# Graph network: the attention's logits with features on the partitions instead of edges

## The reference, cut to what matters

```
x_l = (x @ W_l).reshape(n, H, C)
x_r = (x @ W_r).reshape(n, H, C)
e = (ea @ W_e).reshape(-1, H, C)
m = jax.nn.leaky_relu(x_l[src] + x_r[dst] + e, NEG_SLOPE)
alpha = jnp.einsum('ehc,hc->eh', m, att)
amax = jax.ops.segment_max(alpha, dst, num_segments=n)
expa = jnp.exp(alpha - amax[dst])
denom = jax.ops.segment_sum(expa, dst, num_segments=n)
a = expa / (denom[dst] + 1e-16)
out = jax.ops.segment_sum(x_l[src] * a[:, :, None], dst, num_segments=n)
```

## Time and profile before

| what | us |
|---|---|
| median of the three runs | 2528.77 |
| span of the profiled execution (first to last instruction) | 2249.7 |
| what lies around the span (the median less the span; the profile has no time of its own for the execution) | 279.1 |
| first to last gather of the attention | 984.6 to 2142.2 |
| last logits of the last group done | 2150.4 |

### The profile page before, as it was taken

One profiled execution on the slowest core, in us unless ns is written; L12 is line 12 of the kernel. 1 busy time (PEld: TensorE's weight loads), 2 busy tenths in 40 slices (PEclk: granted clock), 3 DMA queues, 4 the chain that ended last, 5 costly groups with the idle time before them and its releaser, 6 DMA issues. The chain is left out here.

```text
span 2249.7 us, 34161 instructions
## 1 busy us (share of the span) xinstructions
PE 1665.0 (74%) x10041; PEld 1359.7 (60%) x10041; DVE 1504.7 (67%) x3141; ACT 969.8 (43%) x2263; POOL 916.3 (41%) x880
## 2 busy tenths in 40 slices
PE   5566666899799999865667677766777767776756
PEld 2455555655478887634566666666666656666744
DVE  4766666577744342477677777867777867787875
ACT  0355565677455234430234434434434335344535
POOL 1000000000100000037777777777777777777800
PEclk9555555799999999988788988888888898898877
DMA  2100000000034000034333333333343333333211
GB/s 70 60 1 1 1 1 1 8 0 0 29 87 130 27 1 6 14 100 96 92 90 91 97 93 91 92 96 92 87 100 94 86 95 97 91 93 93 60 39 29
DMA packets 134433, 136.86 MB, mean 61 GB/s; under 512 B 28689, under 2 KB 105074, under 8 KB 134258
## 3 DMA queue, kind: packets, MB, share of 16 engines
q0 software_dynamic: 27776, 60.71, 12.2%
q1 hardware_dynamic: 106482, 73.98, 11.5%
HBM read 129.67 MB, written 4.92 MB: 60 GB/s over the span
## 5 line engine op out<-in xcount | busy, mean ns | idle before, releaser
L2112 POOL DMA_INDIRECT rows<-x_l,src x856 | 896.9, 1048 | 292.5 <-issue 260.1
L2180 PE MATMUL psum<-both,node_hot 128*128 128x144 f32 x1712 | 304.1, 332 | 202.0 <-DVE both L2374 175.2
L2180 PEld LDWEIGHTS psum<-both,node_hot 128*128 128x128 f32 x1712 | 264.7, 222 | 229.4 <-issue 197.4
L2127 PE MATMUL psum<-w_e,edges 128*128 128x272 f32 x856 | 323.9, 466 | 56.7 <-DVE z L2287 46.9
L2129 PEld LDWEIGHTS psum<-x_r,hot 128*128 128x128 f32 x1712 | 313.8, 224 | 51.1
L2129 PE MATMUL psum<-x_r,hot 128*128 x1712 | 313.1, 312 | 0.0
L2287 DVE TENSOR_TENSOR z<-psum,rows 128x544 f32<-128x544 f32 x214 | 154.3, 721 | 235.4 <-issue 163.7
L2237 ACT ACTIVATE apart<-iota,minus_rel 128x128 f32<-128x128 f32 x828 | 261.9, 386 | 0.0
L769 ACT ACTIVATE counts<-psum (+1 forms) x181 | 181.5, 1003 | 175.8 <-PE psum L762 112.1
L1145 POOL TENSOR_TENSOR ht<-ht,mix_rows 128x512 f32<-128x512 f32 (+1 forms) x7 | 7.8, 1149 | 587.4 <-ACT mix_rows L1186 587.4
L1260 PE MATMUL psum<-halves,counts 128*128 128x257 f16 (+1 forms) x1725 | 198.1, 277 | 7.4 <-DVE halves L1465 3.9
(11 more groups left out here) (335 smaller groups left out, 2187.3 us busy)
## 6 DMA issues: line engine op xcount, KB each, us to landing
rel_row<-e_rel_rows SPq DMA_DIRECT2D x107, 256.0 KB
edges<-edge_t SPq DMA_DIRECT2D x428, 32.0 KB
rows<-x_l,src POOLq DMA_INDIRECT x856
edge_part<-edge_t SPq DMA_DIRECT2D x40, 320.0 KB, 3.1
x_r<-x_l SPq DMA_DIRECT2D x1, 1632.0 KB
ht<-x SPq DMA_DIRECT2D x6, 256.0 KB, 2.8
new<-e_new_before SPq DMA_DIRECT2D x12, 128.0 KB
new<-e_new_behind SPq DMA_DIRECT2D x12, 128.0 KB
```

Of the source, the lines that this page charges most:

```text
L2112: e.indirect_dma_start(rows[:, g % ring, j * ROW:(j + 1) * ROW], None, k.xl, bass.IndirectOffsetOnAxis(ap=src[:, at:at + 1], axis=0)).then ...
L2127: e.matmul(pair[:, j // 2, :], edges[:, r, :], w_e[:, j:j + 2, :].rearrange("p j f -> p (j f)"), start=True, stop=False)
L2180: final = e.matmul(to, near_hot[:, at, j, :], both[:, at, j, :], start=j % 2 == 0, stop=j % 2 == 1)
```

## The change

Rows of x_l are 128 numbers, the seventeenth columns are gone. x_r is split into three bfloat16 parts whose sum is x_r (`RowParts.split`); the first five blocks are split by GpSimd inside `project`, the others by DVE in steps 0 to 3 of the attention. The logits' sum is made with features on the partitions (128 x 512 in one PSUM bank for each group): PE multiplies x_r's parts with the one-hots, which are bfloat16 now, W_e with the edge features, and the gathered rows with the identity (`join`), which transposes and adds them. ACT writes 0.2 times the sum to `bent` (`slope`), DVE takes the maximum of the two (`bend`), and PE multiplies with a matrix that holds att for one of 16 places (`head_sums`), so that a batch's logits are added up in PSUM as lines at once; `turn_alpha`, `add_rows`, the old `bend` and the old `head_sums` on DVE are gone. The first two blocks of the diff below are PE's, the third is ACT's, the fourth DVE's. `own_logits` moves to steps 5 to 9 and has five instructions instead of four. `minus_rel` is replaced by a scale of -1.

```
                 for t in range(len(due)):
+                    if t < groups:
+                        join(t)
                     if t + 1 < groups:
-                        logits(t + 1)
-                    for piece, turn in ((0, turn_alpha), (1, turn_ends), (2, turn_carries), (5, turn_weights)):
+                        begin(t + 1)
+                    for piece, turn in ((1, turn_ends), (2, turn_carries), (5, turn_weights)):
...
                     for u in due[t]:
                         sum_rows(u)
+                    if t < groups:
+                        head_sums(t)
```

```
+                def begin(g):
...
+                    e.wait_ge(hots.sem, hots.at(g + 1))
+                    if g >= 2:
+                        e.wait_ge(leaky.sem, leaky.at(g - 1))
+                    for j in range(2):
+                        half = slice(j * 2 * P, (j + 1) * 2 * P)
+                        for q in range(3):
+                            e.matmul(z[:, half], row_parts.parts[:, bass.ds(blocks[j], 1), q, :].rearrange("p o f -> p (o f)"),
+                                     hot[:, two, half], start=j + q == 0, stop=False)
+                    e.wait_ge(edge_here[r].sem, edge_here[r].at(2 * lap(g)))
                     for j in range(4):
+                        final = e.matmul(z[:, j * P:(j + 1) * P], w_e[:, j, :], edges[:, r, :], start=False, stop=False)
                     final.then_inc(*products.up())
+                def join(g):
+                    z = k.bank[g % 2]
+                    e.wait_ge(got[g % slots].sem, got[g % slots].at(4 * lap(g)))
+                    for j in range(4):
+                        final = e.matmul(z[:, j * P:(j + 1) * P], rows_at(g)[:, j * P:(j + 1) * P], k.ident[:, :],
+                                         start=False, stop=j == 3)
+                    final.then_inc(*joined.up())
+                def head_sums(g):
...
+                    e.wait_ge(leaky.sem, leaky.at(g + 1))
...
+                    e.matmul(alphas_of(b), k.att_heads[:, low:low + b.lines], bent[:, g % 2, :],
+                             start=c == 0, stop=c == b.n - 1).then_inc(*alphas.up())
```

```
+                def slope(g):
+                    e.wait_ge(joined.sem, joined.at(g + 1))
+                    if g >= 2:
+                        e.wait_ge(alphas.sem, alphas.at(g - 1))
+                    e.activation(bent[:, g % 2, :], k.bank[g % 2], ACT.Copy, scale=NEG_SLOPE).then_inc(*sloped.up())
...
                     for u in (due[t + 1] if t + 1 < len(due) else []):
                         fill(u)
+                    if t < groups:
+                        slope(t)
```

```
                 def bend(g):
+                    e.wait_ge(sloped.sem, sloped.at(g + 1))
+                    e.tensor_tensor(bent[:, g % 2, :], k.bank[g % 2], bent[:, g % 2, :], ALU.max).then_inc(*leaky.up())
...
                     if t + 2 < groups:
                         one_hots(t + 2)
-                    if t < groups:
-                        add_rows(t)
                     for u in due[t]:
...
                         weigh(u)
-                    if t < groups:
-                        bend(t)
                     for u in due[t - 1] if t else []:
                         add(u)
                     if t < groups:
-                        head_sums(t)
-                    if t < cuts:
-                        own_logits(t)
+                        bend(t)
+                    if t + 1 < cuts:
+                        row_parts.split(e, t + 1, split)
+                    if cuts <= t < 2 * cuts:
+                        own_logits(t - cuts)
```

More of the change, by code:

```diff
@@ L1743, with __init__ @@
 class EdgeTables:
-    def __init__(self, k, scope):
+    def __init__(self, k, scope, rows, over):
         s, steps = k.s, 2 * k.s.padded
         self.k, self.steps = k, steps
+        self.first = over - -(-2 * steps // (4 * ROW))
+        self.by_pair = rows[0:1, self.first:over, :].rearrange("o g f -> o (g f)")[:, 0:2 * steps].rearrange(
+            "o (a n v) -> o a n v", a=2, v=2)
         def sb(name, shape, dt=F32):
@@ L1769, in sync, with project @@
             e.dma_start(to, what).then_inc(*self.loaded.up(16))
-def project(k, x, norm, ahead, xr, xl, mean, w_e, tables):
+def project(k, x, norm, ahead, xr, xl, mean, w_e, tables, row_parts):
     s = k.s
@@ L1795, in project @@
         projected, kept, kept_r = k.flag("projected"), k.flag("x_l_kept"), k.flag("x_r_kept")
-        flat = [w[:, j, :, :].rearrange("p h c -> p (h c)") for j in range(3)]
-        both = w[:, 0:2, :, :].rearrange("p j h c -> p (j h c)")
+        split = k.flag("x_r_split")
+        both = raw[:, 0:2, :].rearrange("p j f -> p (j f)")
         with k.nc.Block() as block:
@@ L1965, in schedule, with attention @@
     return slots
-def attention(k, x, h, xr, w_e, acc, rows, own, loops, tables):
+def attention(k, x, h, xr, w_e, acc, rows, own, loops, tables, row_parts):
     s, io, groups = k.s, k.io, k.s.groups
@@ L2047, in lap, with alphas_of @@
             return 16 * (g // slots + 1)
[L2049 to L2050 removed]
+        def alphas_of(b):
+            return k.bank[2 + b.two][0:b.lines, :]
         def by_head(j, b):
@@ L2122, in logits @@
                     e.wait_ge(edge_here[r].sem, edge_here[r].at(2 * lap(g)))
-                    if g >= 2:
-                        e.wait_ge(sums.sem, sums.at(g - 1))
                     for j in range(4):
-                        if j % 2 == 0:
-                            e.matmul(pair[:, j // 2, :], edges[:, r, :], w_e[:, j:j + 2, :].rearrange("p j f -> p (j f)"),
-                                     start=True, stop=False)
-                        final = e.matmul(pair[:, j // 2, j % 2 * ROW:(j % 2 + 1) * ROW], hot[:, two, j * P:(j + 1) * P],
-                                         node_rows[j // 2], start=False, stop=j % 2 == 1)
@@ L2682, in layer3 @@
         acc, w_e = sb("acc", [P, s.nb, D + 2 * HEADS]), sb("w_e", [P, 4, ROW])
-        k.att = sb("att", [P, HEADS, CH])
+        k.att, k.att_heads = sb("att", [P, D]), sb("att_heads", [P, 2 * LINES - HEADS])
         rows = sb("rows", [P, RING, 4 * ROW])
-        tables, loops = EdgeTables(k, scope), OwnLoops(s, rows)
-        project(k, x, norm, ahead, xr, loops.xl, loops.mean, w_e, tables)
+        loops = OwnLoops(s, rows)
+        tables = EdgeTables(k, scope, rows, loops.first)
+        row_parts = RowParts(k, scope, xr, loops.z)
+        project(k, x, norm, ahead, xr, loops.xl, loops.mean, w_e, tables, row_parts)
         ahead.passing.close()
-        attention(k, x, h, xr, w_e, acc, rows, own, loops, tables)
+        attention(k, x, h, xr, w_e, acc, rows, own, loops, tables, row_parts)
         feed_forward(k, x, h, acc, xr, own)
```

156 lines of the change are left out of this document (81 added, 75 removed).

## The result

The changed kernel takes 2580.45 us (median of 4 runs, 2569.47 to 2585.43), the kernel before beside it 2528.13 (2525.51 to 2531.3): a ratio of 1.0198, 95% interval [1.0175, 1.0222]. The forecast was 2533 with a range up to 2577, so it is slower than forecast by 47 us and outside the range.

The account below looks back on a forecast made before the run. The prediction took GpSimd's issuing of gathers, at least 1.252 us each, as the bound. Start +3.5, 160 groups -13.5, groups 182 to 197 +2 and last 16 steps +12.5 gave +4.5, so 2533 us, range 2493 to 2577.

Parts of the forecast that it names:

- Removal on DVE, locks, one-hot: DVE per group: about 4.0 to 2.5 us; new bend no longer locks out gathers, weigh and one-hots (0.45 us) still do.
- -13.5 us for 160 groups: Groups 22 to 181, ten batches: gathers lose 4.0 us per 16 groups to DVE's locks, against 5.35 before.
- PE's 4.24 us: PE's work per group after the change, up from 2.82; fits below the gathers' 5.008 at full clock.
- the hidden wait: PE's head_sums waits for ACT and DVE; ready 2.5 us after join's start, while PE is still in sum_rows.
- steps +1, +2, +5: Steps after a batch, where ACT's fill or PE's turns delay head_sums: 7.6, 5.6 and 8.6 us long.
- consumers 81: PE, ACT and DVE by themselves need 81 us per 16 groups, GpSimd 84, so GpSimd still bounds, narrowly.
- Start, +3.5: Steps 0 to 9: DVE's splits and own_logits hold up gathers, +3.5 us (0 to 8); project's changes 0.
- Groups 182 to 197, +2: Pair steps: a shorter lock per step, 1.6 us instead of 1.95, but steps late: +2 us (-3 to +5).
- The last 16, +12.5: Last 16 steps: the bound leaves GpSimd for the loop PE, ACT, DVE; 111.5 us against 99.1, +12.5 (0 to 18).
- The loop binds: Rival, 20%: PE's clock stays at 0.87, 16 groups take 88.3 us, GpSimd waits for join: +48, 2577.
- Free slot: Rival, 22%: steps get back on time at once, nearly all locks miss the gathers, 160 groups save 48: 2495.
- Locks stay: Rival, 8%: 16-bit one-hot and weigh hold up gathers as much as before, no saving in 160 groups: 2547.

Follow-up runs that it names:

- second execution of the changed kernel: The changed kernel run again, unchanged, on the same chip as the kernel before: 2576.17 us, ratio 1.0175 [1.0088, 1.0263].
- the kernel before again: The kernel before, unchanged, profiled and timed once more: 2525.86 us (8 runs), ratio 0.9994, span 2533.7.

## Why the prediction was wrong

**The step that failed: what bounds the kernel now.** "The sum is made against the profiled execution: its span of 2249.7 and the 279.1 around it" and "GpSimd never waits for anybody". The first was an assumption: only the span and the median were given, and the difference could as well be time inside a usual execution. It was. In those GpSimd waits 290 us for DVE, which waits for PE's semaphores, and 16 groups take 107 us and not 85.5. With the 279 us unexplained, the argument "what lies beside it is free" had no ground, and lowering the gathers' pace made the kernel before faster (0.9879).

**Removal on DVE, locks, one-hot.** The mechanism of the locks held. Of the 21 gathers that began over 0.24 us before the end of the new bend none was held up; of the 28 under weigh all were, and ended 0.82 after it. In the rows of before 76 long gathers ended 0.82 after the old bend. The gathers' busy time fell from 875.6 to 840.0, 36 us, but a gather that is quicker brings nothing where gathers wait for join. The 16-bit one-hot still held the few gathers that began in its first 0.1 us (1.06 us, two of them in the second execution of the changed kernel). The -13.5 us for 160 groups came out as +4.7 (1074.3 to 1079.0).

**PE's 4.24 us, the hidden wait, steps +1, +2, +5, "consumers 81".** Right where semaphores are on time: 4.28, 7.76, 6.13, 9.13, 80.9. In a usual execution they are 6.2, 9.7, 6.6 and 15.0. The prediction said "head_sums can start 2.5 after join's start"; it is 5.24 (1298.50 to 1303.74), for the 2.8 us of the semaphore. That is the new wait, as far as it was argued from the code: the change put two hand-overs from PE into each step's loop (join to slope, head_sums to the next slope but one) where before there was one (the product to add_rows), with PE up to two groups ahead of it.

The lateness alone doesn't make the changed kernel the slower one, since both pay it. It took from the forecast its ground, the bound by the gathers; what the change costs beside it is the difference by stretch below.

**Clock.** Forecast 0.95, measured 0.93.

**Start, +3.5.** 13 us (153.6 to 166.5). **Groups 182 to 197, +2.** 9.6. **The last 16, +12.5.** 4.8. After them, 0: 1.8. With the 4.7 of the 160 groups 34 us, the difference of the two spans, where the forecast had 4.5. The medians differ by 52, and by about 50 when run again, since the profiled execution of before was its slowest (2535.84) and that of after its fastest; by stretch the 34 is thus low, and 18 of the 52 us have no place. In a second execution of the changed kernel (2576.47) the 160 groups take 1086.6, 12 more than before. Why the start and groups 182 to 197 cost 9 and 8 us more than forecast was not tested.

**The rivals.** *The loop binds* named 2577, and GpSimd does wait for join. But it expected 88.3 us for 16 groups from a clock of 0.87; there were 107.9 at 0.93. Its number is near by chance, since the 279 us stood elsewhere in the sum. *Free slot* and *Locks stay* argued about gathers' pace and fell with it; the terms of *Free slot* add up to 2490 to 2493, not to its 2495.

**Open.** Why the semaphores are late: that it goes away with half the indirect gathers is shown, not whether the gathers themselves do it, their packets or their semaphore updates (16 a gather, 70 to 80% of them missing from the record wherever PE's come late), not what any of these have in common with TensorE's semaphores, nor why a join between two gathers is heard at once in one step and not in the next. Nor why one execution of the kernel before had no late one at all; none of over 60 executions since was below 2500 us with that kernel. Every execution here has its span recorded, so it isn't shown either that one without a record would have the delays. At the half clock 2 of the changed kernel's 24 joins were over 0.1 us late, against 160 of 177 at the full clock; in the kernel before again it was 8 of 20 products against 63 of 118. So the half clock doesn't rule them out, and it was not varied by itself.

## What to carry to other kernels

A profile's span that is far from the timed median is a question to settle before any sum: price the difference as unknown time inside the kernel, on the path, until a row shows where it is. Where TensorE hands over to other engines while GpSimd issues indirect gathers, look for late semaphores (some 3 us here) before pricing a loop by busy times, and try such a hand-over a step behind. An engine's short wait ("slope") goes ahead of its long standing work ("fill"): that order alone was worth 2.7%.

## What the hardware showed that was not expected

- TensorE's semaphores came 2.8 us (median, the changed kernel's join) and up to 13 us (the kernel before again) after the recorded end while indirect gathers were issued 1.25 us apart, and 14 ns (median) after it with half as many. Those of ACT and DVE, where recorded, were never over 0.1 us late.
- Half the rows or half the bytes in a gather change its cost on GpSimd little (950 and 982 ns for 981).
- A one-hot of 128x512 from int16 takes 346 ns with 16-bit output (488 with float32).
- At the start of the attention there are steps where PE's matmuls of one group stand up to 1.8 us apart with no wait recorded between them:

```profile
1020.40 0.84 PE L2161 MATMUL psum<-edges,w_e 128*128 128x128 f32 x3
1021.77 0.27 PE L2161 MATMUL psum<-edges,w_e 128*128 128x128 f32 x1 [0.53 <-issue]
1023.88 0.27 PE L2161 MATMUL psum<-edges,w_e 128*128 128x128 f32 x1 [1.83 <-issue]
1024.59 0.37 PE L2161 MATMUL psum<-edges,w_e 128*128 128x128 f32 x1 [0.44 <-issue]
```

They belong to begin, for the group to come. Slope for the group before it started at 1025.50, with the late semaphore of a join that had ended before 1019.4.
